# Relation layers of a graph network on one core: sums by node and relation before the relation weights, with gathered rows as the stationary operand

## What is computed

```python
def _rgcn_layer(x, W, W_root, b, src, dst, edge_type, num_nodes, num_rel):
    h = jnp.einsum('nd,rdf->rnf', x, W)
    msg = h[edge_type, src]
    comb = dst * num_rel + edge_type
    cnt = jax.ops.segment_sum(ones, comb, num_segments=num_nodes * num_rel)
    norm = 1.0 / jnp.clip(cnt[comb], 1.0)
    agg = jax.ops.segment_sum(msg * norm[:, None], dst, num_segments=num_nodes)
    return agg + x @ W_root + b
```

## Time and profile before

| | |
|---|---|
| median of 3 runs | 8774.1 us |
| span of the profiled execution, first to last instruction | 8694.1 us |
| TensorE busy, of the span | 6376.9 us, 73% |
| VectorE busy | 5552.2 us, 64% |
| GpSimd busy | 3238.2 us, 37% |
| ScalarE busy | 1317.8 us, 15% |
| mean granted TensorE clock, share of full speed | 0.789 |

### The profile page before, as it was taken

How to read it: one execution, slowest core, us unless ns; L and a number is a source line. 1 busy time by engine, 2 the same in 40 slices (tenths; PEclk the granted TensorE clock), 3 DMA queues, 4 the chain that set the end, 5 groups by cost and what they waited for, 6 DMA issues and landing times. The chain is left out here.

```text
span 8694.1 us, 138919 instructions
## 1 busy us (share of the span) xinstructions
PE 6376.9 (73%) x36273; PEld 3791.6 (44%) x36274; DVE 5552.2 (64%) x10618; ACT 1317.8 (15%) x3535; POOL 3238.2 (37%) x3402
## 2 busy tenths in 40 slices
PE   7999998734444444449999899986677767667776
PEld 3444446634433443436777567752222223222222
DVE  8888887355555555537777677755555554555556
ACT  0010003100000100012222322221111111111111
POOL 0000000027676776740000000006666664666666
PEclk8999998855555555558999899988878887788877
DMA  0000003522222221111111011111111112111111
GB/s 17 15 18 16 15 15 145 210 73 55 54 51 55 54 55 49 48 32 50 45 45 49 28 53 45 45 50 22 21 21 21 21 21 45 20 22 21 21 21 22
DMA packets 281353, 367.04 MB, mean 42 GB/s; under 512 B 197704, under 2 KB 203578, under 8 KB 281274
## 3 DMA queue, kind: packets, MB, share of 16 engines
q1 hardware_dynamic: 179882, 202.80, 7.3%
q0 software_dynamic: 97792, 142.80, 7.2%
q10 hardware_dynamic: 3600, 20.48, 0.6%
HBM read 309.36 MB, written 56.51 MB: 42 GB/s over the span
## 5 line engine op out<-in xcount | busy, mean ns | idle before, releaser
L1685 POOL DMA_INDIRECT r0s_got<-rel_h,r0s_now x880 | 924.8, 1051 | 2459.4 <-ACT r0s_now L1672 2082.2
L972 POOL DMA_INDIRECT en_got<-edge_q,en_now x1296 | 1294.8, 999 | 413.0 <-issue 368.8
L405 PE MATMUL ps_count<-hot_s,hot_d 128*128 128x512 bf16 (+1 forms) x6160 | 1260.1, 360 | 44.5 <-ACT rows L435 21.8
L1771 PE MATMUL r1s_ps<-r1s_typed,r1s_hot 128*128 128x512 f32 x1760 | 964.8, 700 | 412.1 <-DVE r1s_typed L1722 345.6
L1771 PE MATMUL r0s_ps<-r0s_typed,r0s_hot 128*128 128x512 f32 x1760 | 969.6, 702 | 402.1 <-DVE r0s_typed L1722 331.1
L1685 POOL DMA_INDIRECT r1s_got<-rel_h,r1s_now x880 | 926.2, 1053 | 515.0 <-issue 234.4
L1161 PE MATMUL en_t<-ident,en_got 128*128 128x128 f32 x1296 | 359.3, 433 | 857.5 <-DVE en_got L1055 681.1
L388 DVE TENSOR_SCALAR hot_s<-iota_s,srcm 128x3200 bf16<-128x3200 f16 x880 | 921.4, 1047 | 0.0
L405 PEld LDWEIGHTS ps_count<-hot_s,hot_d 128*128 128x128 bf16 x6160 | 542.1, 98 | 607.4 <-ACT rows L435 72.0
L1771 PEld LDWEIGHTS r1s_ps<-r1s_typed,r1s_hot 128*128 128x128 f32 x1760 | 364.3, 219 | 1011.9 <-DVE r1s_typed L1722 517.8
L1771 PEld LDWEIGHTS r0s_ps<-r0s_typed,r0s_hot 128*128 128x128 f32 x1760 | 364.7, 220 | 1006.3 <-DVE r0s_typed L1722 547.5
(11 more groups left out here) (330 smaller groups left out, 8729.6 us busy)
## 6 DMA issues: line engine op xcount, KB each, us to landing
en_got<-edge_q,en_now POOLq DMA_INDIRECT x1296
count_rows<-rows SPq DMA_DIRECT2D x25, 800.0 KB
c0s_rows<-count_rows SPq DMA_DIRECT2D x25, 800.0 KB, 4.6
count_panels<-c0s_panel ACTq DMA_DIRECT2D x25, 800.0 KB
c1s_rows<-count_rows SPq DMA_DIRECT2D x25, 800.0 KB, 6.1
c1s_panel<-count_panels SPq DMA_DIRECT2D x25, 800.0 KB, 7.6
en_raw<-count_panels SPq DMA_DIRECT2D x25, 800.0 KB
a0s_rows<-count_rows SPq DMA_DIRECT2D x25, 800.0 KB, 5.7
```

The lines of the kernel that those rows point to most:

```text
L405: pe.matmul(ps[:, c:c + wd], hot_d[:, j, :], hot_s[:, j, c:c + wd], start=fresh, stop=True, skip_group_check=True)
L972: pool.indirect_dma_start(out=got[:, i, j, :], out_offset=None, in_=k.q[:, :], in_offset=bass.IndirectOffsetOnAxis(ap=now[i][:, j:j + 1], ...
L1685: pool.indirect_dma_start(out=got[:, j, :], out_offset=None, in_=k.h[:, :], in_offset=bass.IndirectOffsetOnAxis(ap=now[:, j:j + 1], axis=0 ...
L1771: pe.matmul(ps[:, ds(w % 2, 1), :].rearrange("p a c -> p (a c)"), hot[:, j, :], typed[j][:, :, :].rearrange("p r d -> p (r d)"), start=fre ...
```

## The change

`relation_features` and `relation_sums` give way to one block, `relation_layer`.

- The table in DRAM, `rel_table`, now holds the nodes and not the products: 3200 rows of 194 bfloat16 (388 bytes): the float32 features split in three bfloat16 parts of 64, a one, and a zero. VectorE makes the split in three pieces of 9, 9 and 7 windows, SyncE stores each.
- Row numbers are the sources alone (`src_row`), copied for two tiles at a time. A gather waits for `now_ok` alone, once in two gathers, and there are 16 slots in place of 8.
- A tile's one-hot has 512 columns, one for each of 64 nodes times 8 relations, from the keys `dst * 8 + relation`: one VectorE `tensor_scalar` for each tile with two per-partition scalars, float16 in, bfloat16 out. The one-hot of relations and the spread rows are gone.
- TensorE takes the gathered rows as the stationary operand (columns 0 to 127, then 128 to 192) and the one-hot as the moving one: two bfloat16 products of 512 columns for each tile, into two banks. The sums come out with features as partitions and (node, relation) as columns; the column of ones gives the counts.
- Windows have 64 nodes (50 of them, 49 with edges), runs are rounded up to a multiple of 2 tiles and to at least 3 pairs. A new function, `span_tables`, computes this second table of windows once, after `prepare`, in a block of its own.
- ScalarE copies a finished window's two banks to `sums` (two copies of 512 columns). After every second window TensorE multiplies, for each relation, the sums of 128 nodes (stationary, float32, every eighth column of `sums`) with that relation's weights (65 columns, float32): 16 products into `zp`. VectorE then divides by the counts (`average`), adds over relations and writes `z`.
- The root product is made first in the block, 25 small products, and copied by ScalarE to `acc` in four pieces; ScalarE's first row numbers and VectorE's first one-hot come behind that.

The core of the diff:

```diff
+def relation_layer(nc, k, source, weight, root, bias, name):
...
+            with pool.Fori(NT, last_place(pool), SLOTS) as n:
+                for j in range(SLOTS):
+                    if j % GR == 0:
+                        wait_alone(pool, now_ok, n + (j + GR), passed[0])
+                    pool.indirect_dma_start(
+                        out=got[:, j // GR, j % GR, :], out_offset=None, in_=k.rel_table[:, :],
+                        in_offset=bass.IndirectOffsetOnAxis(ap=now[:, j:j + 1], axis=0)).then_inc(gat[j], 16)
...
+                    act.wait_ge(multiplied, at + (3 * GR - SLOTS))
+                    act.activation(now[:, :].rearrange("p (s j) -> p s j", j=GR)[:, ds(pair, 1), :]
+                                   .rearrange("p a j -> p (a j)"), k.src_row[:, ds(t0, GR)],
+                                   ACT.Copy).then_inc(now_ok, GR)
...
+            wait_alone(act, multiplied, last_place(act) + 2 * GR, passed[3])
+            act.sem_inc(now_ok, SLOTS)
+            line_up(V - 1, (V - 1) % 2, last_place(act))
...
+                v.wait_ge(multiplied, at + GR)
+                for j in range(GR):
+                    v.tensor_scalar(hot[:, ds(half, 1), j, :].rearrange("p a c -> p (a c)"), k.rel_iota[:, :],
+                                    k.rel_base[:, ds(w, 1)], k.key8[:, ds(t0 + j, 1)],
+                                    ALU.add, ALU.is_equal).then_inc(spread, 1)
...
+                for j in range(GR):
+                    pe.wait_ge(spread, at + (j + 1))
+                    pe.wait_ge(arrived, at + (j + 1))
+                    for a, (lo, hi) in enumerate(((0, P), (P, P + C))):
+                        last = pe.matmul(ps[s][a][0:hi - lo, :],
+                                         got[:, ds(pair, 1), j, lo:hi].rearrange("p a c -> p (a c)"),
+                                         hot[:, ds(half, 1), j, :].rearrange("p a c -> p (a c)"),
+                                         start=fresh and j == 0, stop=True, skip_group_check=True)
+                    last.then_inc(multiplied, 1)
...
+                for r in range(NREL):
+                    out = zp[:, r // 4, r % 4 * C:(r % 4 + 1) * C]
+                    pe.matmul(out, sums[0][:, :, r], two[:, r, :], start=True, stop=False, skip_group_check=True)
+                    last = pe.matmul(out, sums[1][0:C, :, r], one[:, r, :], start=False, stop=True,
+                                     skip_group_check=True)
```

More of the change, by code:

```diff
@@ new lines, in window @@
+            def window(w, s, least):
+                first, end, place = span(v, w)
+                mark(w, first, place)
+                mark(w, first + GR, place)
+                if least >= 3 and s == 1:
+                    average((w - 3) // 2 if isinstance(w, int) else v.snap((w - 3) // 2))
+                with v.Fori(first + 2 * GR, end, GR) as t0:
+                    mark(w, t0, place)
+            v.wait_ge(kept, len(OCT))
+            every(v, window)
+            average(V // 2 - 1)
@@ L1775, in _ @@
-            with pe.Fori(0, W) as w:
-                first, end, place = window_tiles(pe, k, w)
-                pe.wait_ge(read, w + 1)
-                tiles(w, pe.snap(first + place), True)
-                with pe.Fori(first + G, end, G) as t0:
-                    tiles(w, pe.snap(t0 + place), False)
+            pe.wait_ge(loaded, 16 * 5)
+            for n, (w, m) in enumerate(OCT):
+                if n >= 2:
+                    pe.wait_ge(kept, n - 1)
+                for j in range(m):
+                    last = pe.matmul(rs[n % 2][:, j * D:(j + 1) * D], k.xt[:, (w + j) * P:(w + j + 1) * P],
+                                     wt[:, :], start=True, stop=True, skip_group_check=True)
+                last.then_inc(rooted, 1)
@@ L1784, in store_nodes, with window @@
+            def window(v, s, least):
+                first, end, place = span(pe, v)
+                pe.wait_ge(lined, v + 1)
+                multiply(s, pe.snap(first + place), True)
+                with pe.Fori(first + GR, end, GR) as t0:
+                    multiply(s, pe.snap(t0 + place), False)
+                if least >= 1 and s == 0:
+                    weigh(v)
+            every(pe, window)
+            weigh(V)
 def store_nodes(nc, k, out):
@@ L1832, in build @@
             turn_nodes(nc, k, k.z if n else k.x, ACT.Copy, f"r{n}t")
-            relation_features(nc, k, weight[n], root[n], bias[n], f"r{n}f")
-            relation_sums(nc, k, f"r{n}s")
+            relation_layer(nc, k, k.z if n else k.x, weight[n], root[n], bias[n], f"r{n}s")
         add_and_norm(nc, k, 1.0, "n3")
```

379 lines of the change are left out of this document (223 added, 156 removed).

## The result

The changed kernel takes 9179.9 us (median of 4 runs, 9166.2 to 9195.4), the kernel before 8775.8 (8771.3 to 8782.2): 1.0468 times as long, 95% interval [1.0453, 1.0483]. Slower by 404 us, where 381 us less were forecast, and far outside the range. Every run's time is its span and some 2 us; only the profiled execution of before has a span 80 us under its timed runs. Some 50 of the 80 seem to be in the edge layer, whose gathers go from 1865.7 to 3841.4 there and from 1879.2 to 3905.0 in the profile of after, at unchanged code.

What follows compares the result with a forecast made beforehand. GpSimd's gather loop, disturbed by VectorE, was taken to bound the relation sums. Loops -350, layer starts -72, layer ends +26 and second table +15 gave -381 us: 8774 to 8393 us, range for 8 in 10 8210 to 8640.

Steps and rivals of the forecast that it cites:

- The number and length of gathers: GpSimd in the relation sums: 886 gathers against 880, and 388-byte rows cost no more issue time than 256.
- The stretch: Lengthening of each GpSimd gather by VectorE work beside it: 0.055 us forecast, against 0.109 before.
- Rival 4: Gather's own 0.94 us: the one-hot shuts GpSimd out, a gather costs 1.69 us, total 9014 us; chance 0.09.
- the step headed *TensorE: Relation sums: TensorE needs 42 us for 36 tiles against GpSimd's 47, so it stays covered at no cost.
- the step headed *VectorE: Relation sums: VectorE at 0.52 us a tile against 1.30; slow stretches stay, but 16 slots freed by TensorE cover them.
- 40 us of stalls: Gather loop of a relation layer: 40 of the 175 us of stalls remain, bounds 0 and 175.
- rival 2: Relation sums: TensorE becomes the bound, weight loads of every eighth column at twice 0.337 us; 8638 us, chance 0.10.
- Rival 3: Relation sums: VectorE's slow issue becomes the pace, about 1.55 us a tile, 8763 us; chance 0.12.
- Start of a layer: Weight load to first gather: 26.5 us instead of 62.4, so -36 us a layer, -72 in all.
- End of a layer: Last matmul of the sums to `z`: 14.5 us instead of 2, so +13 us a layer, +26 in all.
- The second table: Block of `span_tables` after `prepare`, repeating its chain: +15 us, hidden by nothing.
- loops: Gather loops of the two relation layers: 1190 us instead of 1365 each, -175 a layer, -350 in all.

Runs made afterwards that it cites:

- after_pause_8: Changed kernel plus a GpSimd memset of 128x8 values behind each gather, on chip 13: 8025.6 us, where the kernel before took 8098.8.

## Why the prediction was wrong

**The number and length of gathers** were right: 886 one-hots, 896 gathers, a mean of 0.955 us, 0.30 us between two in a row. 388 and even 512 bytes cost GpSimd no more than 256 (medians 947 and 944 ns). The stretch was forecast at 0.055 and is 0.955 - 0.944 = 0.011: the one-hot in float16 to bfloat16 disturbs GpSimd five times less than its share of VectorE's time made believe. Rival 4 (0.31 us of stretch or more) is refuted. The one-hot took 0.424 us for 0.45.

**The step that failed** is the one headed *TensorE*: "42 us against GpSimd's 36 x 1.30 = 47: TensorE holds even at the low clock". It costed TensorE's products and not its sequencer. The products were priced right: at the low clock they start 0.43 us apart (8412.07 and 8412.49 in after), 0.86 a tile. But the loop issues four weight loads, four matmuls and some ten register, branch and wait steps a pair. Between the stretches these steps hide at the low clock (granted clock 0.50 from 8409.4 to 8412.4) and set the pace at the high one (1.00 from 8413.0 to 8416.5): there a matmul needs 0.22 us and four of them 0.88, yet pairs follow each other in 1.60 (weight loads at 8413.99 and 8415.59). In a slow stretch each step costs 0.70 us, and one to two tiles pass in some 10 us. The loop took 1602 us (first matmul 7542.6, last 9144.9) for a forecast of 1190. That is 412 a layer, 824 in all, and the whole miss is 787.

**With it fell** the step headed *VectorE*: "slow stretches stay. What changes is what they hold". Half right, and worth most as a lesson. I took the slow issue of the earlier trace rows for VectorE's own and counted VectorE's steps. It is everybody's; before, it showed on VectorE because VectorE had the most steps on the path. In layer 1's sums the register, branch and wait steps recorded go from 1416 to 5051 on TensorE and from 4280 to 2777 on VectorE. The change moved steps from VectorE to TensorE, and the stall moved with them. The cover of 16 slots is useless then, since the engine that frees them is the one that stalls: 40 us of stalls forecast, 512 us of GpSimd's idle time behind row numbers alone. Rivals 2 and 3 each had half of this: TensorE the bound, slow issue the pace. Rival 3's price was wrong because it took the old 1.55 us a tile as the worst case; 1.80 came. And the 0.09 for slower stood on rival 4 alone, while the way it went slower was open in my own.

**The smaller terms held.** Start of a layer: first gather 18.8 us behind the weight load (7520.3 to 7539.1), forecast 26.5. The root products took less, since a pass of the 25 small ones costs 0.21 us, not 0.337; -44 a layer for -36. These are the rows:

```profile
L1860 PE MATMUL r1s_rs<-r1s_wt,xt x50: 421/421/473, 7525.8 to 7536.3; 65*128 65x64 f32 x50
...
L1889 PEld LDWEIGHTS r0s_zp<-r0s_one,r0s_sums x400: 334/335/338, 5994.5 to 7501.6; 65*128 65x128 f32 x134
```

End of a layer: 13.7 us from the last sum's matmul (7491.4) to `z` (7505.1) for 14.5. The weight products with their strided loads cost 0.335 a load, no more than contiguous ones; rival 2's doubling did not come. The second table: first one-hots of the count stage at 81.6 for 63.6, so +18 for +15. Terms against measurement, two layers each: loops 2 x (1602 - 1365) = +474 for -350, starts -87 for -72, ends +23 for +26, table +18 for +15: together +428, where the medians differ by 404 and the two profiles' spans by 493, of which the edge layer's 50 are a part.

**Where the forecast's premise is true**, on a chip without slow steps, its loop is right: in `after_pause_8` (a memset that fits in the 0.30 us between gathers) it goes from 6845.5 to 7981.8, 1136 us for 1190, and the kernel takes 8026. Yet before takes 8099 there: most of what the change was to recover, before's 175 us of stalls a layer, was itself the slow steps. This is an estimate, since before has no trace of its own there: of the 598 us between its spans, 8694 and 8097, the edge layer accounts for some 180, which leaves some 205 for each loop and puts it at 1160 us for 1365, already the gathers' pace. The 0.9% that is left is a single look at each. The change itself was not run on such a chip, and of its relatives there two beat before (8026 and 7990) and two don't (8118 and 8187).

What stays open: why an indirect DMA brings the slow steps, why they come in stretches, in after some 9 to 12 us long and starting every 17 to 30, and whether chips or another lasting condition divides the runs. All times here are of recorded executions, so whether the recording takes part can't be said either. The Trainium skill (NOTIFIC — the notification-queue block, Overflow: three behaviours, one of which stalls the engine) says that the block which writes the records always holds its producers back rather than lose a record inside itself. A stall of every recording engine at once looks like that, and the steps that start together on SyncE, VectorE and ScalarE fit any one thing that serves them in turn; that it is the recording, no run here shows.

## What to carry to other kernels

"Issue" idle time on one engine is not that engine's property: look at the idle ones beside it (before's ScalarE had 884 us of it, nearly all off the path) before you conclude that moving work away cures it. When a change moves work between engines, count the sequencer steps that it puts on the engine which ends last, loads, waits, address registers and branches included, and price them at the slow step of the trace as well as at the fast one. And where a disturbance is in the trace that no code explains, measure on other chips before pricing a change by it: here the change is 4.7% slower where the slow steps are, and where they aren't, versions close to it range from 0.9% faster than before to 1.1% slower.

## What the runs showed of the hardware

- With indirect DMAs in flight, on three of five chips, the sequencers of TensorE, VectorE, ScalarE and SyncE went together through stretches in which a step takes 0.70 us instead of 0.05 (TensorE's wait; 0.017 for SyncE's); before took 8779 to 8787 us there and 8043 to 8099 on the other two. In all 20 traces no step of 0.68 to 0.74 us lies outside the stages with indirect DMAs. Plain DMAs of the same number of 388-byte rows, from GpSimd or SyncE, never did it (7835, 7817 us).
- The 0.30 us behind a gather is usable: a memset of 128x8 in it left the pace at 1.256 us (a gather at 7001.53, the next at 7002.78 in that trace), one of 128x128 made it 1.34.
- A plain DMA of the same size costs GpSimd 0.540 us, an indirect one 0.955.
- A one-hot in float16 with two per-partition scalars, 0.42 us of VectorE, stretched the gather beside it by 0.011 us; the two-input float32 operations before, 0.90 us, by 0.109. The GPSIMD Engine Reference of the Trainium skill (Key points) names both kinds for contention with GpSimd; these means agree with it for the second kind and show next to nothing for the first.
